# A two-layer transformer kernel: five shared-expert tiles placed behind the routed ones, the last stage's first preparation placed inside them, and a new order of the program's first work

## The chip, the cores and the metric

The kernel is one program on one core of a Trainium2 chip. Six instruction streams run beside each other and meet through semaphores: TensorE (PE in the profile, with its weight loads as PEld), VectorE (DVE), ScalarE (ACT), GpSimd (POOL), and SyncE (SP), which here only issues transfers. POOL issues transfers too, the indirect ones. The metric is the device time of one execution in microseconds (us); lower is better.

## What is computed

Two blocks over 4096 tokens of width 256, in fp32. Abbreviated:

```python
x  = L0_attn_x                                    # (8, 512, 256)
xn = _layernorm(x)
x  = x + _L0_attn_ref(xn, ...) + _L0_ffn_ref(xn, ...)
xn = _layernorm(x)
x  = x + _L1_attn_ref(xn, ...) + _L1_ffn_ref(xn, ...)

def _expert(x, w1, b1, w3, b3, w2, b2):
    h = jax.nn.silu((x @ w1 + b1) * (x @ w3 + b3))
    return h @ w2 + b2
# _L0_attn_ref: causal softmax attention, 16 heads of 16
# _L0_ffn_ref: a softmax gate picks 2 of 8 experts per token (hidden size 352),
#   y = sum of the two experts' outputs by their scores, and
    z = _expert(xf, sw1, sb1, sw3, sb3, sw2, sb2)  # the shared expert, all tokens
    return (y + z).reshape(shape)
# _L1_attn_ref: a gated linear recurrence along the sequence
# _L1_ffn_ref: sigmoid gate with groups, 2 of 8 small experts, and a shared MLP
```

## The kernel before

**Three stages, with a barrier of all engines between them.** The first (mix_phase, up to about 487 us) works on 8 blocks of 512 tokens: layernorm, projections, attention, the gate of the first ffn. It stores the normalised tokens (xn_dram) and x plus attention (x_dram in the trace). The second (experts_phase, 488 to 869) does the ffn's experts on tiles of 256 tokens. The third (layer1_phase, from about 872) does the second block on 8 blocks of 512 tokens.

Products are taken as three fp16 products: each operand is split into a high part (ACT rounds it) and a low part (DVE or POOL subtracts), and PE adds high*high, low*high and high*low (lines 113 to 115).

**The start.** For block 0 DVE normalises four groups of 128 tokens (xn, L547), PE transposes them, ACT and DVE split them (xT_hi, xT_lo, L554), and PE projects to q, k, v. The weights wqkv, gate and wout are split ahead of that: DVE's part is wqkv_lo, gate_lo, wout_lo (L685 to L689). q and k go to DRAM and come back stacked (stacks of 16 heads; two transfers' worth of semaphores, half the heads each); then scores (L819), their maximum (L668), exponential, and so on. Meanwhile POOL fills constants (v_aug's ones, L384) and adds the output bias to x (xb, L366).

**The middle stage.** Every engine runs the same skeleton, over_experts, with its own tile function. There are 16 shared tiles (all tokens through the shared expert), then one loop over 8 experts with that expert's routed tiles; with these inputs there are 37. A tile's PE work is: two thirds of the gate and up products (gate_up), the transposes of the next tile's input (x_transposes, L1385, from the buffer xg into a PSUM bank), the last third, and then the output products of the tile before. ACT adds a bias (a), rounds the input transposed (gT_hi) and takes silu; DVE multiplies (prod, L1287), makes the low parts (gT_lo, h_lo) and writes the output (y, L1302), which SP stores to y_dram (L1124).

*Inputs.* A shared tile's xg is a plain load by SP, two tiles ahead. A routed tile's xg is gathered by POOL, two indirect DMAs of 128 tokens each (L1165), from a list of token numbers. DVE copies a tile's two columns of that list to token_now once the gather before has landed; POOL's gather for tile i + 2 waits for that and for tile i's transposes.

*The list (table).* It is made by 64 products in_lane x in_column, one for each 128 (token, choice) pairs: in_lane has a one in the pair's place within 128 slots, in_column the token's number in the column of its slot. POOL writes both for each pair in turn, during the first shared tiles (L1180 and L1181: lanes compared with a position, times the token number). PE multiplies them after 14 shared tiles.

*Weights.* Two buffers. When a new expert begins, SP issues the load of the weights for the expert after next: 704, 256 and 96 KB (L1092 to L1094). Their split into high and low parts (split_in, split_out) lies in the first tile of the expert before. The small biases come after the first tile's output.

*The last stage's weights* (pack) are split in 14 parts beside the shared tiles (pack_part, L1324).

**The last stage.** Its block needs x_dram (to xin), the shared output (to ysh), and each token's two routed rows, gathered from y_dram by POOL in eight indirect DMAs (rows_k, L1670). POOL adds xin and ysh (x, L1677), DVE adds the weighted rows and takes statistics, POOL the inverse deviation, ACT normalises (l_xn, L1720), PE transposes (L2005), ACT and DVE split (l_xT_hi, l_xT_lo, L1849), and PE's products start (L113 on ybank). For blocks 1 to 7 this front work lies beside the products of the block before; for block 0 it stands alone at the start of the stage:

```python
        def pipeline(eng, front, step, tail):

            front(0, 0)
            step(0, 0, False, True)
```

## Time and profile before

| | |
|---|---|
| time, median of 3 runs | 1291.93 us (1289.08 to 1292.2) |
| profiled execution | 1292.68 us, span 1290.9 us, 27101 instructions |
| PE busy (share of the span) | 1128.2 us (87%) |
| PE weight loads | 763.8 us (59%) |
| DVE busy | 904.2 us (70%) |
| ACT busy | 677.7 us (52%) |
| POOL busy | 541.6 us (42%) |
| most time by one kind of wait in the middle stage | gathers of xg, 15.3 us on PE |

Busy is the time in which an engine's datapath runs an instruction; DMA issues of POOL count as busy. The rows further down are lines of the profile and of answers of the trace; "<-" behind the idle time in brackets names what ended it.

### The profile page before, as it was taken

The page shows a single profiled execution, that of the slowest core. Times are in us where ns is not written, and L with a number is a line of the kernel's source. Part 1 is how long each engine was busy: PE and PEld are TensorE (multiplying, and loading weights), DVE is VectorE, ACT ScalarE, POOL GpSimd, SP SyncE. Part 2 cuts the span into 40 slices and gives each one's busy share as a digit, 9 for nine tenths or more (in the row PEclk, how much of TensorE's full clock was granted, in tenths as well). Part 3 has the DMA queues.
Part 4 walks back from the last instruction along what each step waited for, and adds up shares of the span by engine and source line. Part 5 has one row for each costly group of instructions (what it writes and reads, how often), then busy time and mean ns, then how long its engine had stood idle before and what let it go on. Part 6 is the DMA issues. An engine that isn't in the chain of part 4 may idle for free. (4 is left out here: it accounts for less than half of the span.)

```text
span 1290.9 us, 27101 instructions
## 1 busy us (share of the span) xinstructions
PE 1128.2 (87%) x8935; PEld 763.8 (59%) x8967; DVE 904.2 (70%) x2190; ACT 677.7 (52%) x1464; POOL 541.6 (42%) x729
## 2 busy tenths in 40 slices
PE   4688988889889885999999999971999999999998
PEld 2235555455455544998889888860556556556555
DVE  5687887778878835776666666652867867867865
ACT  2156555555555544666565666541554554554553
POOL 4342333323233227992222222215356456456424
...
GB/s 117 88 59 205 106 52 91 74 59 102 72 75 58 43 17 141 164 132 91 118 112 83 115 113 143 118 97 119 115 33 132 132 33 130 130 33 132 96 1 98
DMA packets 97179, 123.62 MB, mean 96 GB/s; under 512 B 14160, under 2 KB 86672, under 8 KB 96080
## 3 DMA queue, kind: packets, MB, share of 16 engines
...
q8 instruction: 42, 0.69, 0.2%
q10 hardware_dynamic: 4096, 0.14, 0.2%
...
## 5 line engine op out<-in xcount | busy, mean ns | idle before, releaser
L458 ACT ACTIVATE p<-bank 128x384 f32<-128x384 f32 (+1 forms) x384 | 193.1, 528 | 197.0 <-PE bank L834 151.0
L668 DVE TENSOR_REDUCE neg_max<-bank 128x1 f16<-128x384 f32 (+3 forms) x352 | 218.7, 641 | 82.5 <-PE bank L822 71.9
L379 POOL TENSOR_SCALAR_AFFINE_SELECT p<-p 128x256 f32<-128x256 f32 x256 | 103.3, 407 | 262.2 <-ACT p L458 260.9
L113 PE MATMUL xbank<-gT_hi,w_hi 128*128 128x256 f16 (+1 forms) x636 | 174.9, 275 | 9.5 <-DVE w_lo L1261 5.8
L115 PE MATMUL xbank<-gT_hi,w_lo 128*128 128x256 f16 (+1 forms) x636 | 174.8, 275 | 0.0
L114 PE MATMUL xbank<-gT_lo,w_hi 128*128 128x256 f16 (+1 forms) x636 | 174.7, 275 | 0.0
L819 PE MATMUL bank<-k_stack,q_stack 96*128 96x384 f16 (+3 forms) x512 | 133.6, 313 | 40.6 <-DVE neg_max L668 29.7
L1165 POOL DMA_INDIRECT xg<-xn_dram,token_now x76 | 72.9, 959 | 196.5 <-PE xbank L1385 144.8
L1213 ACT ACTIVATE a<-xbank,b 128x256 f32<-128x256 f32 x159 | 74.3, 468 | 60.8 <-PE xbank L115 60.4
L834 PE MATMUL bank<-q_stack,k_stack 97*128 97x512 f16 (+1 forms) x256 | 91.3, 361 | 6.3 <-ACT p L458 3.5
L819 PEld LDWEIGHTS bank<-k_stack,q_stack 96*128 96x128 f16 x512 | 46.5, 99 | 80.5 <-DVE neg_max L668 58.3
L1708 POOL TENSOR_TENSOR he_lo<-he_sq,he_hi 128x512 f16<-128x512 f32 x64 | 75.5, 1198 | 42.1 <-ACT he_hi L1794 42.1
L1287 DVE SCALAR_TENSOR_TENSOR prod<-xbank,b,a 128x256 f32<-128x256 f32 x159 | 74.2, 478 | 25.0 <-ACT a L1213 19.7
L113 PE MATMUL xbank<-w_hi,h_hi 128*128 128x256 f16 (+1 forms) x318 | 88.0, 277 | 2.0 <-DVE y L1302 2.0
L115 PE MATMUL xbank<-w_hi,h_lo 128*128 128x256 f16 (+1 forms) x318 | 87.8, 276 | 0.0
L114 PE MATMUL xbank<-w_lo,h_hi 128*128 128x256 f16 (+1 forms) x318 | 87.8, 276 | 0.0
L852 PE MATMUL bank<-p,v_aug 128*32 128x512 f32 (+3 forms) x1024 | 83.1, 443 | 0.8 <-DVE o_rows L648 0.8
L1794 ACT ACTIVATE he_hi<-he_sq 128x512 f16<-128x512 f32 x64 | 39.4, 627 | 83.8 <-DVE he_sq L1932 83.8
L1205 ACT ACTIVATE gT_hi<-xbank 128x512 f16<-128x512 f32 x54 | 32.2, 597 | 93.8 <-PE xbank L115 73.8
L1293 DVE TENSOR_TENSOR h_lo<-h,h_hi 128x256 f16<-128x256 f32 x159 | 66.6, 421 | 19.8 <-ACT h_hi L1222 19.3
L114 PE MATMUL ybank<-l_xT_lo,pack_hi 128*128 128x512 f16 x208 | 79.6, 383 | 0.0
L113 PE MATMUL ybank<-l_xT_hi,pack_hi 128*128 128x512 f16 x208 | 79.5, 382 | 0.0
...
## 6 DMA issues: line engine op xcount, KB each, us to landing
...
xr<-in_x SPq DMA_DIRECT2D x8, 512.0 KB, 7.0
xn_dram<-xn SPq DMA_DIRECT2D x8, 512.0 KB, 3.9
...
```

Of the source, the lines that this page charges most:

```text
L113: pe.matmul(out, hi_a(c), hi_b(c), start=first and x == 0, stop=False)
L114: pe.matmul(out, hi_a(c), lo_b(c), start=False, stop=False)
L115: mm = pe.matmul(out, lo_a(c), hi_b(c), start=False, stop=last and x == n - 1)
L379: pool.affine_select(out=diagonal, in_=diagonal, pattern=[[0, 2], [1, P]], compare_op=ALU.is_ge, fill=0.0, base=0, channel_multiplier=-1). ...
L458: act.activation(p32[:, s // GH % 2, s % GH, cols], s_bank[n][:, 0:cols.stop - cols.start], ACT.Exp).then_inc(p_exp.sem, 1)
L668: dve.tensor_reduce(neg_max[:, g % 2, 0:GH * TT].rearrange("p (h t) -> p h t", t=TT)[:, heads[0]:heads[-1] + 1, j], a_bank[c % 2][:, 0:len ...
L819: pe.matmul(to[:, at * w:(at + 1) * w], q_stack[0:STK, u, h0 + h, j * P:(j + 1) * P], k_stack[0:STK, u, h0 + h, 0:w], start=at == 0, stop= ...
L834: mm = pe.matmul(to[:, 0:S - n * P], k_stack[0:AUG, u, h, n * P:(n + 1) * P], q_stack[0:AUG, u, h, n * P:S], start=True, stop=True)
L852: mm = pe.matmul(out_bank[VW * h:VW * (h + 1), k * P:S], v_aug[:, b % 2, k, GH * (g % NG) + h, :], p32[:, g % 2, h, P_OFF[k]:P_OFF[k] + S ...
L1213: act.activation(a1[0:M, m, :], bank[m][0:M, 0:ETOK], ACT.Identity, bias=b13[0:M, u, m:m + 1]).then_inc(a1_s.sem, 1)
L1287: dve.scalar_tensor_tensor(prod[0:M, m, :], bank[m][0:M, ETOK:2 * ETOK], b13[0:M, u, HM + m:HM + m + 1], a1[0:M, m, :], ALU.add, ALU.mult) ...
L1708: pool.tensor_tensor(he_lo[:, e, :], he_sq[:, e % EB, :], he_hi[:, e, :], ALU.subtract).then_inc(he_lo_s.sem, 1)
```

## The change

Three parts, made together.

**Five shared tiles go behind the routed ones** (TAIL_TILES = 5, HEAD_TILES = 11). The shared expert's weights are loaded a second time for them, as expert E + 1. The last stage's preparation of block 0 is taken out of that stage and written into these tiles, with buffers and semaphores that both stages share (class Front): the loads of xin and ysh are issued behind the last routed tile's store; POOL's addition, the row gathers and the inverse deviation lie among the tail's gathers; DVE's sums behind its tail tiles; PE's transposes behind the last output products. Block 0 only needs shared outputs of tiles 0 and 1. The shared output goes to y_dram, the routed one to a new y_routed_dram. In the routed tiles SP stores tile i in tile i, where it stored i - 1 before, and the weights of the expert after next are issued behind the last store of the expert that ends; the biases are loaded there too.

**The table** gets ten columns more (tail tiles take their inputs through it as well, 74 products of 110 columns where it was 64 of 100) and stands behind 9 shared tiles. POOL writes all in_lane, then 16 of the 64 in_column and the ten for the tail; DVE writes the other 48, six in each of the first eight tiles. The last stage's weights are split in 12 parts. The loop over the head's tiles is written out.

**The start.** wqkv has a semaphore of its own; DVE splits wqkv, then the first xT, then bq, gate and wout; PE begins the first projections after wqkv_lo alone; POOL adds x's bias only after xT_lo, and fills v_aug's ones behind q_low(0, 0), where it did so first; the first four heads' stacks are fetched by themselves.

```diff
+TAIL_TILES = 5
+HEAD_TILES = SHARED_TILES - TAIL_TILES
+ROUTED_SLOTS = SLOTS + (TAIL_TILES - SHARED_TILES) * ETOK
+PLACES = 2 * T // P
+TAIL_PLACES = TAIL_TILES * ETOK // P
+PLACED_BY_DVE = 48
+PLACED_A_TILE = 6
...
+                if b == 0 and half == 0:
+                    fetch_heads(u, slice(0, GH), first_heads_loaded)
+                    fetch_heads(u, slice(GH, 2 * GH), stacks_loaded[half])
+                else:
+                    fetch_heads(u, heads, stacks_loaded[half])
...
             inverse_std(0)
+            pool.wait_ge(w_loaded.sem, w_loaded.at(0))
+            pool.wait_ge(xT_lo_s.sem, xT_lo_s.at(0))
+            x_bias(0)
+            q_low(0, 0)
             pool.memset(v_aug[:, :, :, :, HD:HD + 1], 1.0).then_inc(v_filled.sem, 1)
             pool.memset(v_aug[:, :, :, :, HD + 1:VW], 0.0).then_inc(v_filled.sem, 1)
-            pool.wait_ge(w_loaded.sem, w_loaded.at(0))
-            x_bias(0)
-            for m in range(2):
-                q_low(0, m)
+            q_low(0, 1)
...
             normalise(0, range(TT))
-            dve.wait_ge(w_loaded.sem, w_loaded.at(0))
-
-            dve.tensor_scalar(bq[:, :], bqk[:, 0:2], HD ** -0.5, None, ALU.mult).then_inc(bq_scaled.sem, 1)
             dve.wait_ge(w_hi.sem, 1)
             dve.tensor_tensor(wqkv_lo[:, :, :], wqkv32[:, :, :], wqkv_hi[:, :, :], ALU.subtract).then_inc(w_lo.sem, 1)
+            for c in range(DC):
+                x_low(0, c, first_x[c])
+            dve.wait_ge(w_loaded.sem, w_loaded.at(0))
+            dve.tensor_scalar(bq[:, :], bqk[:, 0:2], HD ** -0.5, None, ALU.mult).then_inc(bq_scaled.sem, 1)
             dve.wait_ge(w_hi.sem, 2)
             dve.tensor_tensor(gate_lo[:, :, :], gate32[:, :, :], gate_hi[:, :, :], ALU.subtract).then_inc(w_lo.sem, 1)
             dve.wait_ge(w_hi.sem, 3)
             dve.tensor_tensor(wout_lo[:, :, :], wout32[:, :, :], wout_hi[:, :, :], ALU.subtract).then_inc(w_lo.sem, 1)
-            for c in range(DC):
-                x_low(0, c, first_x[c])
...
-            pe.wait_ge(w_lo.sem, 3)
+            pe.wait_ge(w_lo.sem, 1)
             for m in range(2):
                 q_products(0, m, first_q[m])
                 k_products(0, m, first_k[m])
             for g in range(2):
                 v_products(0, g, first_v[g])
+            pe.wait_ge(w_lo.sem, 3)
...
-            with eng.Fori(2, SHARED_TILES - AHEAD) as i:
-                tile(i, 0, 0, True)
+            tile(0, 0, None, HEAD)
+            tile(1, 0, 0, HEAD)
+            for i in range(2, HEAD_TILES - AHEAD):
+                tile(i, 0, 0, HEAD)
             table()
...
-            tail(eng.value_load(bounds[0:1, E:E + 1], min_val=MIN_TILES, max_val=ROUTED_TILES) + (SHARED_TILES - 1), 0)
+                        tile(r + HEAD_TILES, 1 - k, 1 - k, ROUTED)
+                    last(2 * half + k + 1, 1 - k, first + HEAD_TILES)
+            after = eng.value_load(bounds[0:1, E:E + 1], min_val=MIN_TILES, max_val=ROUTED_TILES) + HEAD_TILES
+            new_expert(E + 1, 1)
+            for t in range(TAIL_TILES):
+                tile(after + t, 1, min(t, 1), t)
+            tail(after + (TAIL_TILES - 1), 1)
...
+                if is_int(e, E + 1):
+                    sp.wait_ge(y_stored.sem, y_stored.at(HEAD_TILES - 1))
+                    sp.dma_start(front.xin[:, :, :], token_rows(dram["x1"])).then_inc(front.xin_loaded.sem, 16)
+                    sp.dma_start(front.ysh[:, :, :], token_rows(dram["y"])).then_inc(front.xin_loaded.sem, 16)
+                    return
+                load_biases(e + 1, 1 - u)
                 sp.wait_ge(e_loaded.sem, e_loaded.at(e + 1))
                 sp.nop(nofuse=True)
                 sp.wait_ge(e_hi.sem, e_hi.at(e))
@@ -1110,8 +1201,8 @@
                 sp.nop(nofuse=True)
                 load_weights(e + 2, u)
...
+            def store(i, to, at):
                 sp.wait_ge(y_ready.sem, y_ready.at(i))
-                sp.dma_start(dram["y"][bass.ds(i * ETOK, ETOK), :].rearrange("(t p) d -> p t d", p=P),
-                             y[:, :, :]).then_inc(y_stored.sem, 16)
-
-            def tile(i, u, before, ahead, to_split=None):
-                if ahead:
+                sp.dma_start(to[bass.ds(at * ETOK, ETOK), :].rearrange("(t p) d -> p t d", p=P), y[:, :, :]).then_inc(y_stored.sem, 16)
...
+                if stage == ROUTED:
+                    store(i, dram["y_routed"], i - HEAD_TILES)
+                    return
+                if stage not in (HEAD, TURN):
+                    store(i, dram["y"], HEAD_TILES + stage)
...
+                    ins = pool.tensor_scalar(in_lane[:, 2 * t + k, :], lanes[:, :], pos_f[:, 1, t, k:k + 1], None, ALU.is_equal)
+            ins.then_inc(lane_placed.sem, 1)
+            for t in range(PLACED_BY_DVE // 2, T // P):
+                for k in range(2):
+                    ins = pool.tensor_scalar(in_column[:, 2 * t + k, :], lanes[:, 0:columns], pos_f[:, 0, t, k:k + 1],
+                                             ids[:, t:t + 1], ALU.is_equal, ALU.mult)
+            ins.then_inc(column_placed.sem, 1)
+            for k in range(TAIL_PLACES):
+                pool.tensor_scalar(in_column[:, PLACES + k, :], lanes[:, 0:columns], tail_at[:, k:k + 1], tail_ids[:, k:k + 1],
+                                   ALU.is_equal, ALU.mult).then_inc(tail_placed.sem, 1)
+            gather(HEAD_TILES)
...
+            gather(end + (HEAD_TILES + 1))
+            pool.wait_ge(front.xin_loaded.sem, front.xin_loaded.at(0))
+            pool.tensor_tensor(front.x2[:, 0, :, :], front.xin[:, :, :], front.ysh[:, :, :], ALU.add).then_inc(front.x2_base.sem, 1)
+            gather(end + (HEAD_TILES + 2))
+            pool.wait_ge(y_stored.sem, y_stored.at(end + (HEAD_TILES - 1)))
+            pool.wait_ge(front.slot_s.sem, front.slot_s.at(0))
+            pool.nop(nofuse=True)
+            gather_rows(0)
+            gather(end + (HEAD_TILES + 3))
+            gather_rows(1)
+            gather(end + (HEAD_TILES + 4))
+            gather_rows(2)
+            gather_rows(3)
...
+                if stage == HEAD and i < PLACED_BY_DVE // PLACED_A_TILE:
+                    place(i)
+                if stage in (HEAD, TURN) and not is_int(i, 0):
+                    pack_part(i - 1)
+                elif stage in range(2):
+                    pack_part(HEAD_TILES - 1 + stage)
+                elif stage == 2:
+                    first_sums(0)
+                elif stage == 3:
+                    first_sums(1)
+                    first_sums(2)
...
+                for n in range(PLACED_A_TILE * i, PLACED_A_TILE * (i + 1)):
+                    dve.tensor_scalar(in_column[:, n, :], lanes_half[:, 0:ROUTED_SLOTS // P], pos_f[:, 0, n // 2, n % 2:n % 2 + 1],
+                                      ids[:, n // 2:n // 2 + 1], ALU.is_equal, ALU.mult).then_inc(placed.sem, 1)
...
+            def first_sums(t):
+                dve.wait_ge(front.slot_s.sem, front.slot_s.at(0))
+                dve.wait_ge(front.x2_base.sem, front.x2_base.at(0))
+                dve.wait_ge(front.gathered[t].sem, front.gathered[t].at(0))
+                for k in range(2):
+                    if k:
+                        dve.wait_ge(row_sum.sem, 2 * t + 1)
+                    dve.scalar_tensor_tensor(front.x2[:, 0, t, :], front.rows_k[:, t, k, :], front.wk[:, t, k:k + 1], front.x2[:, 0, t, :],
+                                             ALU.mult, ALU.add).then_inc(row_sum.sem, 1)
+                dve.wait_ge(row_sum.sem, 2 * t + 2)
+                dve.bn_stats(front.stats[:, t, :], front.x2[:, 0, t, :]).then_inc(stats_s.sem, 1)
...
+            def tail(i, u):
+                out(i, u)
+                pe.wait_ge(front.xn_ready.sem, front.xn_ready.at(0))
+                for c in range(DC):
+                    for t in range(TT):
+                        mm = pe.transpose(front_bank[c][:, t * P:(t + 1) * P], front.xn[:, t, c * P:(c + 1) * P], identf[:, :])
+                    mm.then_inc(front.xT_psum.sem, 1)
...
-PACK_PARTS = SHARED_TILES - AHEAD
+PACK_PARTS = HEAD_TILES + 1
...
-                "y": nc.dram_tensor("y_dram", (MAX_TILES * ETOK, D), F32).ap(),
+                "y": nc.dram_tensor("y_dram", (T, D), F32).ap(),
+                "y_routed": nc.dram_tensor("y_routed_dram", (ROUTED_TILES * ETOK, D), F32).ap(),
...
-        return np.concatenate([shared[None], routed, routed[-1:], routed[-1:]])
+        return np.concatenate([shared[None], routed, shared[None], shared[None]])
```

The order of POOL's instructions at the end of the middle stage. Before, from the last gather of a routed tile (L1165) through the barrier to the addition:

```order
L1165 DMA xg<-xn_dram,token_now 128x256 [waits token_now_s]
L1165 DMA xg<-xn_dram,token_now 128x256
L1185 REGISTER_ALU
L1185 COMPARE_AND_BRANCH
L988 UNCONDITIONAL_BRANCH
L1657 UNCONDITIONAL_BRANCH [waits barrier_Pool_Activation_PE_DVE_SP_gather]
L1659 MEMSET l_minus_half 128x4
L1660 MEMSET nothing 128x4
L1670 DMA rows_k<-y_dram,slot 128x256 [waits slot_s,half_filled,x2_sum]
L1670 DMA rows_k<-y_dram,slot 128x256 x7
L1677 TENSOR_TENSOR x<-xin,ysh 128x1024 [waits l1_y_ready,xin_loaded]
```

Now the same place, from the gather of the second tail tile (L1267 is the gather's line now):

```order
L1267 DMA xg<-xn_dram,token_now 128x256 [waits token_now_s]
L1267 DMA xg<-xn_dram,token_now 128x256
L1310 TENSOR_TENSOR x<-xin,ysh 128x1024 [waits xin_loaded]
L1263 REGISTER_ALU
L1264 REGISTER_ALU [waits gT_psum]
L1267 DMA xg<-xn_dram,token_now 128x256 [waits token_now_s]
L1267 DMA xg<-xn_dram,token_now 128x256
L1312 ISA
L1305 DMA rows_k<-y_routed_dram,slot 128x256 [waits y_stored,slot_s]
L1305 DMA rows_k<-y_routed_dram,slot 128x256
```

The addition, which stood behind the barrier and all row gathers, now stands between the gathers for the second and the third tail tile, and the row gathers follow the third tile's.

SP at a change of expert. Before, the weights (L1092 to L1094) come first, then the store (L1124) of the last tile of the expert that ends, then the biases:

```order
L1108 REGISTER_ALU [waits e_loaded]
L1092 ISA [waits e_hi,e_lo]
L1092 DMA w_32<-in_w 128x2x704
L1093 ISA
L1093 DMA w_32<-in_w 128x2x256
L1094 ISA
L1094 DMA w_32<-in_w 96x256
L1123 REGISTER_ALU
L1124 ISA [waits y_ready]
L1124 DMA y_dram<-y 128x2x256
L1099 ISA [waits y_ready]
L1099 DMA b<-in_b 128x6
```

Now:

```order
L1215 ISA [waits y_ready]
L1215 DMA y_routed_dram<-y 128x2x256
L1152 REGISTER_ALU
L1152 COMPARE_AND_BRANCH
...
L1184 ISA
L1184 DMA b<-in_b 128x6
L1185 ISA
L1185 DMA b<-in_b 128x256
L1197 ISA
L1199 REGISTER_ALU [waits e_loaded]
L1178 ISA [waits e_hi,e_lo]
L1178 DMA w_32<-in_w 128x2x704
```

The store of the ending expert's last tile now stands ahead of the weights and waits for that tile's y_ready.

DVE in a head tile. Before, one turn of the loop over shared tiles:

```order
L1287 SCALAR_TENSOR_TENSOR prod<-xbank,b,a 128x256 [waits h_hi_s]
...
L1280 TENSOR_TENSOR gT_lo<-xbank,gT_hi 128x512 [waits gT_hi_s]
...
L1287 SCALAR_TENSOR_TENSOR prod<-xbank,b,a 96x256 [waits h_hi_s]
L1293 TENSOR_TENSOR h_lo<-h,h_hi 128x256 [waits h_hi_s] x2
L1293 TENSOR_TENSOR h_lo<-h,h_hi 96x256 [waits h_hi_s]
...
L1302 TENSOR_TENSOR y<-xbank,b 128x256 [waits y_stored]
L1302 TENSOR_TENSOR y<-xbank,b 128x256
...
L1324 TENSOR_TENSOR pack_lo<-pack,pack_hi 128x587
```

Now, tile 1:

```order
L1442 SCALAR_TENSOR_TENSOR prod<-xbank,b,a 128x256 [waits h_hi_s,a1_s] x2
L1435 TENSOR_TENSOR gT_lo<-xbank,gT_hi 128x512 [waits gT_hi_s]
L1442 SCALAR_TENSOR_TENSOR prod<-xbank,b,a 96x256 [waits h_hi_s,a1_s]
L1448 TENSOR_TENSOR h_lo<-h,h_hi 128x256 [waits h_hi_s] x2
L1448 TENSOR_TENSOR h_lo<-h,h_hi 96x256 [waits h_hi_s]
L1457 TENSOR_TENSOR y<-xbank,b 128x256 [waits y_stored,y_psum]
L1457 TENSOR_TENSOR y<-xbank,b 128x256
L1499 TENSOR_SCALAR in_column<-lanes_half,pos_f,ids 128x110 x6
L1492 TENSOR_TENSOR pack_lo<-pack,pack_hi 128x684 [waits pack_hi_s]
```

Six placements stand between the tile's output and the pack part.

## Rows read from the trace of the kernel before

**Rows 1.** Windows: busy time of PE, PEld, DVE, ACT, POOL; granted clock; DMA share; GB/s:
```profile
528.00:584.00 56.00, 56.00 (x516) 51.77 (x514) 39.34 (x88) 37.06 (x98) 55.17 (x79) 1.00 0.46 133
...
600.00:859.00 259.00, 241.84 (x2177) 218.12 (x2176) 169.26 (x411) 157.07 (x407) 70.24 (x75) 1.00 0.38 115
...
858.00:862.00 4.00, 4.00 (x24) 3.28 (x22) 1.80 (x4) 1.68 (x4) 0.00 (x0) 0.57 0.10 20
...
876.00:878.00 2.00, 0.00 (x0) 0.00 (x0) 0.13 (x2) 0.00 (x0) 0.95 (x1) 0.50 1.04 355
```

**Rows 2.** Timeline around the barrier: start, busy us, engine, line, operation, [idle before <- releaser]:
```profile
868.77 0.76 DVE L1302 TENSOR_TENSOR y<-xbank,b 128x256 f32<-128x256 f32 x2 [3.00 <-PE xbank L115]
...
873.97 0.43 SPq L1634 DMA_DIRECT2D xin<-x_dram  x1
...
886.75 2.35 POOL L1677 TENSOR_TENSOR x<-xin,ysh 128x1024 f32<-128x1024 f32 x1
...
898.58 1.97 PE L2005 MATMUL ybank<-identf,l_xn 128*128 128x128 f32 x8 [29.94 <-ACT l_xn L1720]
...
901.96 0.19 PE L113 MATMUL ybank<-pack_hi,l_xT_hi 128*128 128x8 f16 x1 [1.42 <-DVE l_xT_lo L1849]
```

**Rows 3.** Timeline, PE: transposes of tile inputs in the middle stage:
```profile
541.27 0.60 PE L1385 MATMUL xbank<-identf,xg 128*128 128x128 f32 x4
...
547.61 0.60 PE L1385 MATMUL xbank<-identf,xg 128*128 128x128 f32 x4
...
848.60 0.60 PE L1385 MATMUL xbank<-identf,xg 128*128 128x128 f32 x4
...
857.36 0.66 PE L1385 MATMUL xbank<-identf,xg 128*128 128x128 f32 x4 [2.26 <-DMA xg<-xn_dram,token_now]
```

**Rows 4.** List of waits, PE: total us, count, longest:
```profile
PE xbank L1385 <- DMA xg<-xn_dram,token_now: 15.3, 10, 2.3
```

**Rows 5.** Timeline of the start, PE and DVE:
```profile
20.39 0.58 PE L113 MATMUL bank<-xT_hi,wqkv_hi 128*128 128x512 f16 x1 [3.91 <-DVE xT_lo L554]
...
35.37 1.38 DVE L547 TENSOR_SCALAR xn<-xr,mv,rstd 128x256 f32<-128x256 f32 x4 [1.48 <-issue]
...
37.97 0.59 PE L819 MATMUL bank<-k_stack,q_stack 96*128 96x128 f16 x4 [6.43 <-DMA k_stack<-qk_hi_dram]
...
39.02 0.69 DVE L668 TENSOR_REDUCE neg_max<-bank 128x4 f16<-128x512 f32 x1 [2.28 <-remote]
```

**Rows 6.** Timeline, POOL and SP, at the last change of expert:
```profile
844.84 0.95 POOL L1165 DMA_INDIRECT xg<-xn_dram,token_now  x1 [0.30 <-issue]
...
850.57 0.40 SPq L1092 DMA_DIRECT2D w<-in_w  x1
...
851.65 0.95 POOL L1165 DMA_INDIRECT xg<-xn_dram,token_now  x1 [0.30 <-issue]
...
854.64 0.40 SPq L1124 DMA_DIRECT2D y_dram<-y  x1
```

**Rows 7.** DMA issues: KB each, median us from issue to landing:
```profile
xin<-x_dram SPq DMA_DIRECT2D x8, 512.0 KB, 9.6
```

**Rows 8.** Two lines of POOL in the middle stage: min/median/max ns, and when:
```profile
L1181 POOL TENSOR_SCALAR in_column<-lanes,pos_f,ids x64: 691/698/2471, 493.7 to 582.5; 128x100 f16<-128x100 f32 x64
L1180 POOL TENSOR_SCALAR in_lane<-lanes,pos_f x64: 589/595/1187, 493.1 to 581.9; 128x128 f16<-128x128 f32 x64
```

**Rows 9.** Timeline, DVE and POOL, operations beside each other:
```profile
11.57 2.88 DVE L547 TENSOR_SCALAR xn<-xr,mv,rstd 128x256 f32<-128x256 f32 x4 [1.50 <-issue]
11.58 1.76 POOL L384 MEMSET v_aug<- 128x1920 f32 x1
...
14.63 3.78 POOL L366 TENSOR_TENSOR xb<-xr,bout_row 128x1024 f32<-128x1024 f32 x1 [1.28 <-DVE xn L547]
...
16.11 2.33 DVE L687 TENSOR_TENSOR gate_lo<-gate,gate_hi 128x16 f16<-128x16 f32 x1
...
547.00 1.39 POOL L1181 TENSOR_SCALAR in_column<-lanes,pos_f,ids 128x100 f16<-128x100 f32 x1
```

373 lines of the change are left out of this document (229 added, 144 removed).

## The prediction

> **What bounds the kernel now.** I read the busy time by windows first, then the timeline around each barrier between stages, then the waits, then the queues of SP and POOL. TensorE (PE) is the engine to follow: from 600 to 859 us it is busy 241.84 of 259 us, at a full granted clock [rows 1]. Three gaps stand out.
>
> The largest is the barrier between the middle and the last stage. The last tile's output leaves DVE at 869.5 (868.77 and 0.76), the first product of the last stage runs at 901.96, and between them PE does only the eight transposes at 898.58 [rows 2]. The chain in that gap: loads of xin and ysh from 873.97, eight gathers on POOL, the addition on POOL at 886.75, sums, statistics, normalisation, transposes. Little of it needs PE, and all of it starts behind the barrier.
>
> The second is in the routed tiles. An undisturbed tile takes 6.34 us (541.27 to 547.61, from one tile's input transposes to the next's); at a change of expert it is 8.76 (848.60 to 857.36), with PE idle for a gather [rows 3]. All such waits sum to 15.3 us [rows 4]. The third is the start: the first projection at 20.39, the first scores at 37.97 after a wait of 6.43 for the stacks [rows 5].
>
> **The sum** is made against the profiled execution, 1292.7 us (span 1290.9), which lies 0.8 above the median of the runs shown, 1291.9.
>
> **Term 1, the barrier: -15.8 us.** Let X be the time of a tile's input transposes. In the kernel before, the last X (857.36) is 44.6 us ahead of the last stage's first product (901.96) [rows 2, 3]. In the changed kernel five shared tiles stand there. The inputs of the first two come as before; the third is the trouble. POOL's order, shown above, puts the addition x<-xin,ysh between the gather for the second tail tile and that for the third. The addition waits for xin and ysh, and SP issues those behind the store of the last routed tile. A store comes 6.04 us after the X of its tile (848.60 to 854.64) [rows 3, 6]; with 0.4 for its issue and some 1.3 for a register load and the waits, the loads go out at X + 7.7. In the kernel before, DMA ran at 355 GB/s from 876 on, 2 us behind the issue at 873.97; at that rate the second of 512 KB each has landed 5.3 us after the first is issued [rows 1, 2]. The median in the last stage, 9.6, is with other traffic and is my upper end [rows 7]. So the addition starts at X + 13 and ends at X + 15.4 (2.35), the third tile's two gathers take 2.2 to issue and land 1.9 later, at X + 19.5 instead of X + 6.34: PE waits 13.1 us. What is queued behind the addition on POOL is that gather alone; DVE stands too, since it names a tile's tokens only when the gather ahead has landed. PE's clock falls: after 2.26 us of idle time the granted clock was 0.57 in 858 to 862 [rows 1, 3]. I add 1.9 for half speed over 3.8 us.
>
> The rest of the tail: 8.2 to the fourth X (with that 1.9), 6.3 to the fifth, 6.3 for one more tile, then what followed the last X before, 857.36 to 869.5, is 12.2, then transposes and split, 898.58 to 901.96, 3.4; these three are 21.9 [rows 2, 3]. Sums, gathered rows and statistics lie beside tiles 3 to 5. From the X that answers to 857.36: 6.6 + 19.5 + 8.2 + 6.3 + 21.9 = 62.5; less five tiles gone from the head, 31.7, it is 30.8 against 44.6; and that X comes 2.0 sooner by term 2. Together -15.8. Ends: -30.8 with no late gather, -11.5 with loads landing in 9.6.
>
> **Term 2, the changes of expert: -11 us.** Weights for a later expert (704, 256 and 96 KB) are issued from 850.57 on, between the two gathers, the second of which ends its issue at 852.60. It landed at 857.36, 4.8 later; in the tile before, 2.8 were enough (845.79 to 848.60) [rows 3, 6]. SP now stores an expert's last tile before it loads weights, so they go out at X + 9.6 instead of X + 2.0. The delayed gather (issue ends X + 4.0) is alone. The next one ends its issue at X + 10 and is wanted at X + 12.7; its data are ahead of most of the weights. One case is in term 1; the others sum to 15.3 - 2.3 = 13.0, and I leave 0.3 to each of seven: -11. Ends: 0, if the next gather is hit as hard; -14.9, all of PE's idle time in 600 to 859 less that one case.
>
> **Term 3, the head: +13 us.** DVE now places six columns in each of eight head tiles. In 528 to 584 it is busy 39.34 of 56 us, 4.45 a tile, so 1.9 are free [rows 1]. No row has this operation; clean, it lies near the 0.16 of a 128x2 operation and the 0.4 of a 128x256 one, say 0.2, and six would fit. But POOL works there without a break, in operations of 0.595 and 0.698 (medians) [rows 8], and rows show each engine held by the other: the 128x16 gate_lo took 2.33 us on DVE and ended with POOL's xb, while xb took 3.78 instead of its usual 2.35 behind DVE's wqkv_lo; four xn took 2.88 beside a memset of POOL, and 1.38 without [rows 5, 9]. gate_lo was queued right behind wqkv_lo, yet POOL's waiting operation went first. So each placement waits for one operation of POOL: 0.6, 3.6 for six. With 0.1 for the larger pack part DVE has 4.45 + 3.6 + 0.1 = 8.15 against 6.34: +1.8 in each of the seven tiles in which POOL still works, 12.7. Ends: 0 if they slip in; 0.78 each (0.59 and their own 0.19) are 4.7, +2.9 a tile, 20 us.
>
> The Trainium skill ("SBUF — State Buffer", Who interferes with whom) says that GpSimd and a VectorE operation in a two-port mode, which tensor_scalar can enter, exclude each other for a whole instruction. It speaks against this edit, and by it the six would cost the upper end. The same section says so of VectorE operations with two SBUF inputs while GpSimd reads SBUF; pack_lo agrees (POOL's operation beside it took 1.39 where the median is 0.698) [rows 8, 9].
>
> **Term 4, the table: +0.5 us,** for ten more matmuls. POOL has 64 lanes and 26 columns left: 64 x 0.595 + 26 x 0.698 x 1.1 = 58, and 6 for being held once a tile, from 493.1 to 557 [rows 8]. PE is through nine head tiles at 557.6 (547.61 + 6.34 to the X in the ninth, 3.6 to its end), or 13 later by term 3: no wait. Without term 3 it would be 2 us (0 to 8).
>
> **Term 5, the start: -6.2 us.** xn no longer meets POOL's memset (-1.5), and xT_lo no longer stands behind gate_lo (2.33) and wout_lo: the projection starts at 16.4 instead of 20.39 [rows 5, 9]. The first four heads are fetched by themselves, half the bytes, so that scores could start 7 us sooner; but DVE has the second block's xn first, which ended at 36.75 (35.37 and 1.38) and moves with the start to 32.75, where the first maximum ran at 39.02 [rows 5]. Ends: -3 and -8. POOL's placing of v_aug's ones behind the first q_low is covered by the v products; uncovered it costs its 1.76 [rows 9]. The shared weights' second split was made before too, unused; DVE's four more slot operations lie beside the first weights' load, and cost 0.7 uncovered.
>
> Sum: 1292.7 - 15.8 - 11 + 13 + 0.5 - 6.2 = 1273.2; less 0.8 for the median: **1272.4 us**.
>
> **Rivals.** (A) The placements slip in between POOL's operations. 1272.4 - 13 + 2 = 1261.4. For it: they are short, and POOL may not hold the port all the time. Against it: all the held rows [rows 9]. Chance 0.22.
>
> (B) The third tail gather isn't late, so that PE never waits there: 1272.4 - 15 = 1257.4. Against it: POOL is in order, and the loads can't go out sooner. Chance 0.10.
>
> (C) The gain at the changes of expert doesn't come, since the weights hit the next gather: that ends its issue 0.4 us behind the first weights' issue, the old one 2.0 us behind. 1272.4 + 13 = 1285.4. Chance 0.12. The Trainium skill ("DMA: Bandwidth & Descriptors", Queues, rings and completion order) says that each DMA engine takes the queues in turn, packet by packet; by it a gather on one queue is not stuck behind another's weights, and moving them wins little, as in C. The 4.8 us against 2.8 do not fit that well [rows 3, 6].
>
> (D) Slower: with DVE as the head's bound PE idles some 1.8 us in each tile, near the 2.26 after which the clock fell [rows 1, 3]. A tile at half speed is 12.7 us of PE, so seven cost 44 in place of 13: 1303.6. It ends above the time before once five of the seven run cold. Against it: the shorter idle times in 600 to 859 left the clock at 1.00 [rows 1]. Chance 0.06.
>
> The forecast has the other 0.50; its own range is 1264 to 1280.
>
> **How the numbers follow.** The range takes in A, B and C and leaves out D and what lies beyond: 1256 to 1287. Under 0.3% (3.9 us) no change can be told. Faster: the forecast, A, B and half of C, 0.88; same 0.07; slower 0.05.
>
> **What would show it.** In the changed profile: one wait of PE of 12 to 14 us for xg, two tiles behind the last routed one, ended by a gather that stands on POOL behind x<-xin,ysh; head intervals of some 8 us, with placements on DVE of 0.5 us or more (A: 0.2, and 6.34); waits for xg in the routed tiles of some 3 us in all; the last stage's first product some 4 us behind the last tile's output; the first projection at 16.4, the first maximum near 33. What would make the prediction wrong is above all the price of a placement, then the weights' collision.

## The result and the profile after

The changed kernel takes 1292.25 us (median of 20 runs, 1287.3 to 1297.74), the kernel before 1287.12 (20 runs, 1283.17 to 1292.52): ratio 1.0038, interval 1.0024 to 1.0051. It is slower by 0.4%, where 1.5% faster was forecast. Measured again beside some of its variants it was 1292.05, ratio 1.0022 (1.0007 to 1.0037).

The page of the changed kernel, its span and engines:

```profile
span 1290.6 us, 26808 instructions
PE 1138.7 (88%) x8941; PEld 773.1 (60%) x8973; DVE 913.0 (71%) x2242; ACT 677.8 (53%) x1462; POOL 526.0 (41%) x700
```

The span is that of the profile before, 1290.9. This is chance: the profile before came from an execution at the slow end of its kernel's range (1292.68 us), and a second one (below) has 1281.9. I therefore compare two profiles of each; the second of the changed kernel has a span of 1290.3. The list of waits on PE in the changed kernel:

```profile
PE xbank L1598 <- DMA xg<-xn_dram,token_now: 31.3, 12, 12.8
...
PE xbank L120 <- DVE y L1457: 3.9, 1, 3.9
PE xbank L1652 <- POOL in_column L1295: 3.9, 1, 3.9
```

The 29.94 us before the last stage's transposes [rows 2] are gone, but the waits for xg have gone from 15.3 [rows 4] to 31.3, the wait for in_column (3.9) is new, and the longest for y has grown from 2.0 to 3.9. The marks between the stages are the transposes of tile inputs, first of the kernel before (timeline, PE: first tile; last shared tile), then of the changed one (first tile; last head tile; last routed tile; first tail tile):

```profile
491.10 0.90 PE L1385 MATMUL xbank<-identf,xg 128*128 128x128 f32 x3 [7.21 <-DMA xg<-xn_dram]
...
595.46 0.60 PE L1385 MATMUL xbank<-identf,xg 128*128 128x128 f32 x4
```

```profile
484.76 1.11 PE L1598 MATMUL xbank<-identf,xg 128*128 128x128 f32 x4 [6.79 <-DMA xg<-xn_dram]
...
563.90 0.60 PE L1598 MATMUL xbank<-identf,xg 128*128 128x128 f32 x4
...
826.04 0.60 PE L1598 MATMUL xbank<-identf,xg 128*128 128x128 f32 x4
...
832.38 0.60 PE L1598 MATMUL xbank<-identf,xg 128*128 128x128 f32 x4
```

The marks have to be counted. Both kernels have 53 tiles, and a tile's input takes four transposes. The kernel before has four transposes too many: its last routed tile also transposes a buffer that no tile uses, and that is the mark at 857.36 [rows 3]. All transposes of tile inputs, of the kernel before and of the changed one (count; min/median/max ns; first and last):

```profile
L1385 PE MATMUL xbank<-identf,xg x216: 272/273/473, 491.1 to 857.7; 128*128 128x128 f32 x108
...
L1598 PE MATMUL xbank<-identf,xg x212: 272/273/478, 484.8 to 877.5; 128*128 128x128 f32 x106
```

So the last routed tile's own inputs are transposed at 848.60 before [rows 3] and at 826.04 now; 857.36 answers to 832.38, the first tail tile's.

Differences of such marks, in us (two profiles of each kernel; the forecast is that of the prediction's terms, sorted by stage). Five tiles of 6.34, 31.7 us, are taken from the head before and from the tail after:

| stretch | before | changed | forecast | measured |
|---|---|---|---|---|
| start to first tile | 491.1, 485.5 | 484.8, 482.7 | -6.2 | -4.6 |
| first tile to last head tile | 72.7, 70.8 | 79.1, 79.2 | +13.5 | +7.4 |
| last head tile to last routed tile | 253.1, 254.8 | 262.1, 262.9 | -11.0 | +8.6 |
| last routed tile's inputs to the last stage's first product | 53.4, 50.5 | 40.9, 40.0 | -15.8 | -11.5 |
| last stage | 388.9, 388.6 | 392.0, 393.9 | 0 | +4.2 |
| sum | | | -19.5 | +4.1 |

Most of the miss of 23.6 us is in the routed tiles (19.6). The barrier won 11.5 of its 15.8.

**The tail's stall.** Timeline of PE, SP and POOL around the third tail tile of the changed kernel:

```profile
841.88 0.81 PE L1598 MATMUL xbank<-identf,xg 128*128 128x128 f32 x4 [3.00 <-DMA xg<-xn_dram,token_now]
...
851.13 0.40 SPq L1193 DMA_DIRECT2D xin<-x_dram  x1
...
856.42 2.34 POOL L1310 TENSOR_TENSOR x<-xin,ysh 128x1024 f32<-128x1024 f32 x1 [20.42 <-DMA ysh<-y_dram]
858.90 0.96 POOL L1267 DMA_INDIRECT xg<-xn_dram,token_now  x1
...
862.89 1.11 PE L1598 MATMUL xbank<-identf,xg 128*128 128x128 f32 x4 [12.80 <-DMA xg<-xn_dram,token_now]
```

This is the chain as forecast: the addition waits for the late loads, the gather (858.90) stands behind it, PE waits 12.80 us (forecast 13.1). All five gaps from the last routed tile's transposes through the tail are 6.3, 9.5, 21.0, 8.0 and 6.3 us.

**The head and the table.** DVE's placements in a head tile, their durations from first start to last, POOL's last placements, the table's products and their window (the column behind POOL is the granted clock):

```profile
509.08 1.42 DVE L1499 TENSOR_SCALAR in_column<-lanes_half,pos_f,ids 128x110 f16<-128x110 f16 x6
...
L1499 DVE TENSOR_SCALAR in_column<-lanes_half,pos_f,ids x48: 296/305/472, 503.7 to 548.6; 128x110 f16<-128x110 f16 x48
...
547.54 7.70 POOL L1295 TENSOR_SCALAR in_column<-lanes,tail_at,tail_ids 128x110 f16<-128x110 f32 x8
...
555.49 2.73 PE L1652 MATMUL xbank<-in_column,in_lane 128*128 128x110 f16 x28 [3.88 <-POOL in_column L1295]
...
555.00:561.00 6.00, 5.41 (x74) 5.28 (x74) 0.06 (x1) 0.00 (x0) 0.24 (x1) 0.72 0.39 94
```

Six placements take 1.42 us, 0.24 each from start to start, with POOL busy throughout. From the third on, the head tiles take 6.3 to 6.5 us, as before the change. But POOL ends only at 555.24, PE stood ready 3.88 earlier, and then runs the table's products at a granted clock of 0.72.

**A change of expert.** POOL's gather for the second tail tile, and the weights beside it:

```profile
833.81 0.94 POOL L1267 DMA_INDIRECT xg<-xn_dram,token_now  x1 [3.76 <-PE xbank L1598]
835.06 0.95 POOL L1267 DMA_INDIRECT xg<-xn_dram,token_now  x1 [0.30 <-issue]
...
835.57 0.38 SPq L1178 DMA_DIRECT2D w<-in_w  x1
```

The gather's issue ends at 836.01; its tile is transposed at 841.88, 5.9 us later, where 2.8 is enough when nothing flies beside it.

In the loop over the experts PE waits 15.5 us for gathers now (31.3 less 12.8 and 3.0), 13.0 before (15.3 less 2.3). That is 2.5 of the 8.6 us in the table's third row. The rest is on PE itself, behind the long waits. Timeline of PE and the stretch behind it, first in the changed kernel, then before the change (last column but two: the granted clock):

```profile
733.58 1.12 PE L1598 MATMUL xbank<-identf,xg 128*128 128x128 f32 x4 [3.16 <-DMA xg<-xn_dram,token_now]
...
733.58:742.00 8.42, 7.93 (x58) 7.09 (x59) 4.90 (x12) 4.09 (x11) 1.89 (x2) 0.83 0.11 34
```

```profile
664.85 0.66 PE L1385 MATMUL xbank<-identf,xg 128*128 128x128 f32 x4 [2.27 <-DMA xg<-xn_dram,token_now]
...
664.85:671.24 6.39, 6.39 (x59) 5.90 (x59) 4.37 (x12) 3.26 (x9) 1.89 (x2) 1.00 0.22 65
```

After waits of 3.16, 3.34 and 3.08 us the next tile took 8.4, 9.1 and 8.1 us, at granted clocks of 0.83, 0.70 and 0.79. In the first profile of the kernel before, no wait in this loop is longer than 2.27, and the tile behind that one took 6.39 at 1.00.

**The end of the tail and the last stage's start.** DVE's last statistics, the last tile's output products, the first product of the last stage, SP's load of a bias, ACT, and the next product of PE:

```profile
888.10 0.38 DVE L1523 BATCH_NORM_AGGREGATE l_mv<-l_stats 128x2 f32<-128x6 f32 x4
...
890.86 0.39 PE L120 MATMUL xbank<-w_hi,h_hi 128*128 128x256 f16 x1 [3.90 <-DVE y L1457]
...
898.62 0.17 PE L120 MATMUL ybank<-pack_hi,l_xT_hi 128*128 128x8 f16 x1 [2.03 <-PEq L1049]
...
899.46 0.42 SPq L1838 DMA_DIRECT2D neg_bz<-in_bias  x1
...
902.21 1.28 ACT L1960 ACT_TABLE_LOAD   x1 [4.99 <-DVE neg_bz L2009]
...
903.76 0.39 PE L120 MATMUL ybank<-l_xT_hi,pack_hi 128*128 128x512 f16 x1 [0.24 <-ACT l_sc L1960]
```

The preparation no longer covers the small loads that the last stage still issues behind its barrier: ACT waits 4.99 us for neg_bz, which DVE scales once it is loaded. The second block's transposes follow the first product by 43.3 and 43.8 us in the changed kernel's two profiles, by 40.65 in both of the kernel before.

**The start.** First projection, first maximum of scores:

```profile
16.48 0.58 PE L113 MATMUL bank<-xT_hi,wqkv_hi 128*128 128x512 f16 x1 [1.50 <-DVE gate_lo L699]
```

```profile
16.48 0.58 PE L120 MATMUL bank<-xT_hi,wqkv_hi 128*128 128x512 f16 x1 [1.50 <-DVE gate_lo L706]
...
31.68 1.28 DVE L686 TENSOR_REDUCE neg_max<-bank 128x4 f16<-128x512 f32 x2
```

(the first fence is the start's edit alone, the second the changed kernel). Forecast were 16.4 and near 33, from 20.39 and 39.02 [rows 5].

### The profile page after: what moved, and what is told of

Its sections match the earlier page's. It is cut to its first block and busy times, and to the rows that moved or that the text cites. A ratio compares the mean times of both kernels' runs of the same rounds, so it can differ in the third digit from the quotient of the medians.

```text
span 1290.6 us, 26808 instructions
## 1 busy us (share of the span) xinstructions
PE 1138.7 (88%) x8941; PEld 773.1 (60%) x8973; DVE 913.0 (71%) x2242; ACT 677.8 (53%) x1462; POOL 526.0 (41%) x700
## 5 line engine op out<-in xcount | busy, mean ns | idle before, releaser
L1267 POOL DMA_INDIRECT xg<-xn_dram,token_now x84 | 80.5, 959 | 211.0 <-PE xbank L1598 152.0
L1448 DVE TENSOR_TENSOR h_lo<-h,h_hi 128x256 f16<-128x256 f32 x159 | 66.9, 424 | 19.9 <-ACT h_hi L1363 19.0
L120 PEld LDWEIGHTS xbank<-gT_hi,w_hi 128*128 128x128 f16 (+1 forms) x636 | 69.2, 109 | 19.0 <-issue 8.3
```

The lines of the kernel that those rows point to most:

```text
L120: pe.matmul(out, hi_a(c), hi_b(c), start=first and x == 0, stop=False)
L1267: pool.indirect_dma_start(xg[:, half, :], None, dram["xn"], bass.IndirectOffsetOnAxis(token_now[:, half:half + 1], 0)).then_inc(gathered.s ...
```

## The experiments

All ratios are to the kernel before, timed beside each.

**The kernels themselves again.** No edit.

> The kernel before once more, for a second profile. Theory (the first stage's length varies from run to run by some us): the first tile transposes of the middle stage start elsewhere than at 491.10, by up to 6 us. Rival (it is constant, and the start's edit is worth the full 12 us between 491.1 and 478.9 in its own run): they start at 491 within 0.5.

Span 1281.9, time 1283.63. Its first and last shared tiles and its last routed one:

```profile
485.51 1.11 PE L1385 MATMUL xbank<-identf,xg 128*128 128x128 f32 x4 [7.81 <-DMA xg<-xn_dram]
...
587.99 0.60 PE L1385 MATMUL xbank<-identf,xg 128*128 128x128 f32 x4
...
842.75 0.60 PE L1385 MATMUL xbank<-identf,xg 128*128 128x128 f32 x4
```

The first stage does vary, by 5.6 us between two executions of one kernel, and a single pair of profiles can't tell a difference of that size.

> The changed kernel once more, for its time beside the runs of its variants and for a second profile. Theory (an execution's first stage and its late gathers vary by some us, and so does the time from one set of runs to another): between 1284 and 1293 us, with a wait of 12 to 13.5 us for xg in the tail, a wait of 3.9 to 6 for in_column, and 14 to 19 us for the other gathers. Rival (the 1292 is a constant of the kernel): within 1 us of 1292.3, and the other gathers at 18 us or more.

1292.05 us (ratio 1.0022, 1.0007 to 1.0037), in its profile 12.8 us for the tail's gather, 6.0 for in_column, 17.7 for the other gathers. The time is as constant as the rival said, the rest within both.

**Loads of xin and ysh early.**

```diff
-                    (in new_expert, for E + 1: wait for y_stored, load xin, load ysh)
 def last(e, u, first):
     if is_int(e, 0):
         store(HEAD_TILES - 1, dram["y"], HEAD_TILES - 1)
+        sp.wait_ge(y_stored.sem, y_stored.at(HEAD_TILES - 1))
+        sp.dma_start(front.xin[:, :, :], token_rows(dram["x1"])).then_inc(front.xin_loaded.sem, 16)
+        sp.dma_start(front.ysh[:, :, :], token_rows(dram["y"])).then_inc(front.xin_loaded.sem, 16)
```

> The changed kernel with one edit: SP issues the loads of xin and ysh right behind the store of the last head tile, some 260 us sooner. Theory (late loads hold the addition, the addition holds the third tail gather in POOL's order): PE's wait of 12.8 us in the tail is gone, the idle time before the addition (20.4 us) too, and the clock stays at 1.00 there; the kernel is 13 to 16 us faster than the changed one, about 1277. Rival (the row gathers or the store of the last routed tile, which the third gather's neighbours also need, hold POOL anyway): the addition goes early but PE still waits more than 6 us within the tail, and the gain is under 7 us.

1279.4 us, ratio 0.993 (0.990 to 0.996): 13 below the changed kernel. The five runs spread from 1272.27 to 1281.84, and the profile is of one at 1272.71. The 12.8 us are gone. What is late next, one tile further (timeline, POOL and PE):

```profile
839.73 0.94 POOL L1305 DMA_INDIRECT rows_k<-y_routed_dram,slot  x1 [5.74 <-DMA y_routed_dram<-y]
...
842.34 1.75 POOL L1267 DMA_INDIRECT xg<-xn_dram,token_now  x1 [0.31 <-issue]
...
847.20 1.12 PE L1598 MATMUL xbank<-identf,xg 128*128 128x128 f32 x4 [4.06 <-DMA xg<-xn_dram,token_now]
```

The first row gather waits for the last routed tile's store, and the fourth tail gather stands behind it: the rival's mechanism, with 4.06 us in place of its 6.

**The addition one gather later.**

```diff
-            (wait for xin_loaded, then the addition x<-xin,ysh)
             gather(end + (HEAD_TILES + 2))
+            (wait for xin_loaded, then the addition x<-xin,ysh)
```

> The changed kernel with one edit: the addition x<-xin,ysh stands behind the third tail gather instead of ahead of it; the loads are as late as before. Theory: the third gather comes in time; the fourth is held in its place until the addition's end, so the wait on PE moves one tile back and shrinks by about a tile, 6 to 8 us instead of 12.8. Rival (the transfers of the tail are slow by themselves): the third gather still lands late.

1280.16 us in one run. The third gather comes in time, the wait moves one tile back:

```profile
846.75 2.34 POOL L1311 TENSOR_TENSOR x<-xin,ysh 128x1024 f32<-128x1024 f32 x1 [9.98 <-DMA ysh<-y_dram]
...
855.68 1.11 PE L1598 MATMUL xbank<-identf,xg 128*128 128x128 f32 x4 [9.70 <-DMA xg<-xn_dram,token_now]
```

9.7 us, more than the 6 to 8 expected, since two row gathers (2.5 us) stand between the addition and that gather. POOL's order sets which tile waits; with the run before it the chain is shown. The time is 12 us below the changed kernel, though the wait shrank by 3: one run doesn't settle what the rest is.

**The start's edit alone**, on the kernel before (its diff is the start's part of the diff above).

> The kernel before with the start's edit alone (wqkv's own semaphore, the new order on DVE, PE and POOL, the first four heads' stacks fetched by themselves). Theory: the first stage ends 6.3 us sooner and nothing later takes it back: 6 us faster than before (ratio 0.995). Rival (a later wait absorbs it, as at the first shared weights' load): under 2 us.

1279.82 us, ratio 0.9955 (0.9936 to 0.9975). Its gain of 5.8 us (3 to 8 by the interval) stays to the end. So the other two parts of the change cost some 9 to 11 us together.

**Few weights.** Inside the loop over experts only one of 128 partitions of each weight is loaded.

```diff
-                load_weights(e + 2, u)
+                few_weights(e + 2, u)      # the same three transfers, partition 0 alone
```

> The changed kernel, but inside the loop over experts each weights load moves only one partition's rows (so experts 2 to 8 and the tail compute with stale weights; the semaphores, splits and products are all there). Theory (weights in flight slow the gather issued beside them): PE's waits for xg in the routed tiles, 18.5 us in the changed kernel, fall under 4 us, and with the clock's share the time falls by some 14 to 20 us. Rival (the gathers at a change of expert are late for another reason, such as the token names that DVE copies behind its weight splits): the waits stay above 12 us.

1267.72 us, ratio 0.9846 (0.9819 to 0.9874), 24 us below the changed kernel, more than the 14 to 20 expected. Waits for xg:

```profile
PE xbank L1604 <- DMA xg<-xn_dram,token_now: 16.0, 5, 13.2
```

2.8 us outside the tail's long one, where the changed kernel has 18.5, and from the last head tile to the last routed tile it is 243.1 us where the changed kernel has 262.1. DVE's splits and token names are all still there, so the rival is out: the weights in flight are what makes the gathers late.

**Weights after a gather.**

```diff
                 sp.wait_ge(e_lo.sem, e_lo.at(e))
                 sp.nop(nofuse=True)
+                sp.wait_ge(gathered.sem, gathered.at(at["first"] + AHEAD))
+                sp.nop(nofuse=True)
                 load_weights(e + 2, u)
```

> The changed kernel with one edit: at a change of expert SP waits until the gather issued in the expert's first tile has landed, and only then issues the weights of the expert after next. Theory (weights in flight slow a gather whose issue ends beside theirs): the weights then fly between two gathers; PE's waits for xg in the routed tiles fall from 18.5 us to under 8, 8 to 12 us faster than the changed kernel. Rival (any place of the loads hits some gather, since they fly for about as long as the gap): the waits stay above 13 us and the time within 3 us.

1281.33 us, ratio 0.9961 (0.9938 to 0.9985); waits 11.2 outside the long one (24.1 less 12.9). But this run doesn't test what it should: the wait named a gather that had landed already. The weights still went out beside the next gather, 0.23 us ahead of the end of its issue at 825.31 where it was 0.44 in the changed kernel:

```profile
825.08 0.38 SPq L1181 DMA_DIRECT2D w<-in_w  x1
```

That 11 us of time go with it was not foreseen, and the shift is not shown to be their cause. The four variants that leave the loop over the experts as it is (loads early, the addition later, and two below: seven placements, placements from fp32) have 13.6 to 15.4 us of these waits and 255.2 to 259.3 us from the last head tile to the last routed tile; this run has 11.2 and 254.7, the changed kernel 18.5 and 17.7, 262.1 and 262.9. So 3 to 7 us of the changed kernel's loop are gone whenever something else in the program is moved. With one gather later:

```diff
-                sp.wait_ge(gathered.sem, gathered.at(at["first"] + AHEAD))
+                sp.wait_ge(gathered.sem, gathered.at(at["first"] + AHEAD + 1))
```

> The changed kernel with SP's weights loads waiting for the gather one later than in the run on weights after the gather: that wait named a gather that had landed already (its issue ended 5.7 us ahead of the weights), so the weights still went out beside the next one. Now they wait for that next one. Theory (weights in flight slow the gather issued beside them): the waits for xg outside the tail's long one fall from 11 to 18 us to under 6, 6 to 12 us faster than the changed kernel beside it. Rival (any place hits some gather): they stay above 11.

1275.23 us, ratio 0.9905 (0.9874 to 0.9936), 17 us below the changed kernel beside it:

```profile
PE xbank L1603 <- DMA xg<-xn_dram,token_now: 19.1, 9, 13.9
```

5.2 us outside the long one, within the theory's 6; the gain is larger than its 6 to 12. From the last head tile to the last routed tile it is 249.3 us, 13 below the changed kernel and 6 to 10 below the four variants just named.

**Weights ahead of the biases.**

```diff
-                load_biases(e + 1, 1 - u)
                 (waits)
                 load_weights(e + 2, u)
+                load_biases(e + 1, 1 - u)
```

> The changed kernel with the two small bias loads behind the weights at a change of expert, so that the weights go out 1.2 to 1.4 us earlier, 1.4 us or more ahead of the end of the gather's issue. Theory (the earlier the weights go out ahead of the gather's end, the longer the gather takes): the gather lands 1 us later still or stays as late, the waits outside the tail's long one are 18 us or more, and the time is that of the changed kernel or up to 5 us more. Rival (the phase is only shifted, the weights are then through sooner): the waits fall under 13 us.

This run and the next were timed in a set in which the kernel before took 1316.17 us (a block of the last stage takes 52 us there, elsewhere 48.3), so that only ratios count. Ratio 0.9936 (0.9912 to 0.996), waits 12.8 us outside the long one (25.8 less 13.0). The rival was right: earlier was not worse. What moves these waits between 11 and 18 us stays open: the phase of weights and gather is a guess that no run isolates.

**The start's edit with weights waiting for the gather in flight**, on the kernel before.

```diff
                 sp.wait_ge(e_lo.sem, e_lo.at(e))
                 sp.nop(nofuse=True)
+                sp.wait_ge(gathered.sem, gathered.at(at["first"] + AHEAD))
+                sp.nop(nofuse=True)
                 load_weights(e + 2, u)
```

> The kernel before with the start's edit, and with the weights loads waiting for the gather that is in flight at the change of expert (no tail tiles). Theory (weights in flight slow the gather beside them, whatever the rest): PE's waits for xg fall from 15 us to under 6, 8 to 12 us below the start alone, about 1269; all_mended at 1255 then owes some 14 us to the tail tiles with the front inside them. Rival (the waits come back at the next gather): over 10 us of waits, within 3 us of the start alone.

Ratio 0.9896 (0.9856 to 0.9936) against 0.9955 for the start alone, intervals that just touch; the waits are 12.8 us, the rival's side:

```profile
PE xbank L1403 <- DMA xg<-xn_dram,token_now: 12.8, 11, 3.5
```

The theory's fall to under 6 us of waits didn't come (the start alone has 14.4). Whether a wait that does keep weights and gathers apart wins as much without tail tiles stays open.

**Seven placements a tile on DVE.**

```diff
-PLACED_BY_DVE = 48
-PLACED_A_TILE = 6
+PLACED_BY_DVE = 56
+PLACED_A_TILE = 7
```

> The changed kernel with seven placements a head tile on DVE instead of six, so that POOL places 8 columns instead of 16. Theory (a placement on DVE takes 0.24 us, POOL's list ends at 555.2 when PE stood ready at 551.6): POOL ends 5.9 us sooner, PE's wait of 3.9 for in_column is gone, and the head tiles stay at 6.34: 4 us faster than the changed kernel, 6 with the clock. Rival (DVE is at its limit, busy 42.3 of 45 us in the head): the head tiles grow to 6.5 or more and eat it.

1283.1 us, ratio 0.9958 (0.9933 to 0.9983). The wait for in_column is gone, the head tiles stay at 6.34, and from the transposes that PE runs in the ninth tile to those of the last head tile, with the table between them, it is 10.8 us (542.90 to 553.66) instead of 16.2:

```profile
546.79 3.37 PE L1652 MATMUL xbank<-in_column,in_lane 128*128 128x110 f16 x64
...
553.66 0.60 PE L1598 MATMUL xbank<-identf,xg 128*128 128x128 f32 x4
```

That is 5.4 us, as the theory had it with the clock: the 74 products now take 3.9 us (546.79 to 550.66), where they took 5.4 (555.49 to 560.9), at a granted clock of 1.00 instead of 0.68. The rest of the 9 us is in the loop over the experts (257.3 us, 15.4 of late gathers), which this edit doesn't touch; it isn't shown to be a gain of the placements.

**Placements from fp32.**

```diff
-dve.tensor_scalar(in_column[:, n, :], lanes_half[:, 0:ROUTED_SLOTS // P], ...
+dve.tensor_scalar(in_column[:, n, :], lanes[:, 0:ROUTED_SLOTS // P], ...
```

> The changed kernel with DVE's placements reading the fp32 lanes instead of the fp16 copy. Theory (it is the fp16 input that lets them slip in beside POOL; the held rows of the kernel before all read fp32): each takes 0.5 us or more and the head tiles grow above 7 us. Rival (the type does not matter, the held rows were the exception): 0.25 to 0.35 us, head tiles within 0.2 of 6.34.

1285.91 us in one run; the tiles stay at 6.34, durations (min/median/max):

```profile
L1499 DVE TENSOR_SCALAR in_column<-lanes,pos_f,ids x48: 320/332/470, 500.5 to 545.4; 128x110 f16<-128x110 f32 x48
```

The type is worth 0.03 us. The theory fell.

**All mended.** Early loads, weights after the next gather, seven placements, and two further edits:

```diff
             gather(end + (HEAD_TILES + 2))
+            gather(end + (HEAD_TILES + 3))
             (wait for y_stored and slot_s)
             gather_rows(0)
-            gather(end + (HEAD_TILES + 3))
-            gather_rows(1)
             gather(end + (HEAD_TILES + 4))
+            gather_rows(1)
             gather_rows(2)
             gather_rows(3)
...
         (SP, last, behind the store of the last head tile)
+                    sp.dma_start(front.bias[:, :], w["bias"]).then_inc(front.loaded.sem, 16)
+                    sp.dma_start(front.corr[:, :], w["corr"].partition_broadcast(P)).then_inc(front.loaded.sem, 16)
+                    sp.dma_start(front.neg_bz[:, :], w["bias"][:, BZ:BZ + DC]).then_inc(front.loaded.sem, 16)
```

> The changed kernel with all mended: xin and ysh loaded behind the last head tile, row gathers behind the fourth and fifth tail gathers, weights behind the next gather, seven placements on DVE, the last stage's biases loaded behind the head. Theory (each stall has its own cause): the gains add, 13 (tail) + 8 (weights) + 4 to 6 (table) + 2.5 (biases) = 28 to 30 us below the changed kernel, about 1258. Rival (they share one bound, the transfers): less than 20 us together.

1254.89 us, ratio 0.9727 (0.970 to 0.9754): 2.7% faster than the kernel before, 37 us below the changed one, where 28 to 30 were expected. The three single edits measured 13, 17 and 9 us, so the gains about add; each of the three holds some of the 3 to 7 us named above. Waits for xg, the last tail tile's transposes, and the last stage's first product:

```profile
PE xbank L1610 <- DMA xg<-xn_dram,token_now: 8.0, 12, 2.3
```

```profile
841.40 0.60 PE L1610 MATMUL xbank<-identf,xg 128*128 128x128 f32 x4
...
863.00 0.17 PE L120 MATMUL ybank<-pack_hi,l_xT_hi 128*128 128x8 f16 x1 [2.42 <-PEq L1053]
```

From the last routed tile's inputs (808.2) to that product it is 54.8 us, 23.1 with the five tiles taken off, where the kernel before has 53.4 and 50.5: some 29 us less, close to the prediction's own end for this term, -30.8 with no late gather. From first product to second transposes it is 40.7, as before the change. From the last head tile to the last routed tile it is 252.3 us, no longer than before the change (253.1, 254.8), but no shorter either.

> The same with DVE's last sums and statistics behind the fourth tail tile's output instead of ahead of the last tile's third product. Theory (they hold up the last tile's DVE work, so that PE waits 3.9 us for y): that wait is gone but the statistics come later, and the last stage's first product comes within 1 us of where it was. Rival (the statistics have slack): 2 to 4 us faster.

```diff
-                if stage == TAIL_TILES - 1:      # ahead of the last tile's third product
-                    first_sums(3)
-                    first_statistics()
                 (third product, low parts, total_y(i - 1))
+                if stage == TAIL_TILES - 1:
+                    first_sums(3)
+                    first_statistics()
```

1255.48 us, ratio 0.9736 (0.9707 to 0.9765): no difference. PE's wait for y falls from 4.1 to 2.6, its transposes wait 2.0 for l_xn instead, and the first product comes at 862.0, within 1 us of 863.0. The theory's part that the wait would be gone is half right.

## Why the prediction was wrong

**The changes of expert** are the step that failed, with 19.6 us of the miss of 23.6: "The next one ends its issue at X + 10 and is wanted at X + 12.7; its data are ahead of most of the weights." The times held (X here is 826.04, the issue ended at 836.01, the weights went out at X + 9.5). The claim on the data didn't: the gather took 5.9 us from the end of its issue to its tile's transposes, and the term of -11 us measured +8.6. This was rival C's mechanism, at 0.12, but C had the gain at nothing, not a loss. The new place is worse than the old one: the waits grew by 2.5 us and three of them passed 3 us, and behind those the tiles ran at granted clocks of 0.70 to 0.83, which the term left out. That weights in flight are the cause is shown by the run with few weights. Of the 8.6 us, 3 to 7 are gone in variants with the same loop, for a reason that stays open; none of them makes it the gain that was forecast.

The Trainium skill ("DMA: Bandwidth & Descriptors", Queues, rings and completion order) has each DMA engine take the queues in turn, packet by packet. By it moving the weights wins little, and it won nothing. Whether taking turns is what delays the gather, no run shows; what they show is the delay, 5.9 us against 2.8, and 17 us won by taking the weights out of the gather's way.

**The head.** "So each placement waits for one operation of POOL: 0.6, 3.6 for six" failed: 0.24 each, and the head tiles didn't grow. Rival A's mechanism, at 0.22, held here, and it made the miss 6.1 us smaller. The rows of held operations [rows 9] were true, but not the price of an operation of this kind. The input's type is not the reason; what is stays open. The Trainium skill ("SBUF — State Buffer", Who interferes with whom) has the two engines exclude each other for a whole instruction when VectorE's is in a two-port mode. No row shows the mode of the placements; the price of 0.6 or 0.78 each that the prediction took from it isn't there.

**The table** was mis-sized: +0.5, or 2 (0 to 8) once the head tiles stay short, against 6.3 in the first profile (16.16 from tile to tile, less 9.84 before) and 8.4 in the second, with 6.0 us of waiting. POOL's list took 67.3 us (487.94 to 555.24) where 64 were reckoned. Its medians, 0.599 and 0.735, are as reckoned or below; it was held for 9.9 us beyond them, not 6. POOL's operations beside DVE's h_lo and pack_lo took 1.22 and 1.53 (507.19, 510.21), those beside six placements 0.61 and 0.66. PE was ready at 551.6, by then sooner than POOL, since the start and the short tiles had brought it forward. And PE's idle time cost its clock (0.72). The run with seven placements shows 5.4 of it to be POOL's lateness and the clock.

**The barrier** had the right mechanism and nearly the right sum. From the transposes that answer to 857.36, those at 832.38, to the first product 62.5 us were forecast and 66.2 measured. The stall itself was 12.8 for 13.1. The missing 3.7 are: 2.9 of a late gather for the second tail tile (9.5 for 6.6; the weights again); 1.5 in the third tile's step, 21.0 for 19.5, as the loads went out at X + 9.3 and not 7.7 (X is 841.88 there); less 0.7 in the rest. In that rest is the tail's end, forecast as 21.9 (one more tile, then what followed the last X before, then transposes and split) and measured as 21.4 (877.18 to 898.62), 21.6 in all_mended. So DVE's sums and statistics, POOL's inverse deviation and ACT's normalisation were hidden, as forecast.

**The last stage** had no term at all. Its small loads had been covered by the preparation that was moved away: 2.7 to 3.1 us, gone in all_mended, where they are issued early. A further 0.5 to 3 us in its later blocks stayed in the changed kernel and all_mended; I didn't find their cause.

**The start** was right within its noise: -6.2 forecast, 5.8 measured alone, 4.6 between the pairs of profiles, while the two of the kernel before differ by 5.6.

**The base** was 1291.9 from three runs, and 1287.1 over 20. That was luck: the time of 1292.25 is 19.9 us from the forecast's 1272.4, but the change itself missed by 24.6 (5.1 slower where 19.5 faster was forecast).

A reading of the clock was loose too. The prediction took 2.26 us of idle time as what makes the clock fall (0.57 in 858 to 862), for term 1 and for rival D. In the same profile PE was idle for 2.27 us before 664.85 and ran the next tile at 1.00.

So A's and C's mechanisms both came true, which I had only as alternatives. Together they would still be 1272.4 - 11 + 13 = 1274.4. The sign changed because the changes of expert lost where C had them even, and the table, the second tail tile's gather and the last stage came on top.
